# Score banks, GpSimd's share and the weights' sums in a feed-forward, attention, feed-forward block

## The chip, the cores and the metric

The kernel runs on one core of a Trainium2 chip. A core has TensorE (PE, matmuls into PSUM, with weight loads shown as PEld), VectorE (DVE), ScalarE (ACT), GpSimd (POOL) and SyncE (SP, which here issues DMAs). Each works through its own instructions in order and waits on semaphores for the others. The metric is the device time of one execution in microseconds, as the median of several runs.

## What is computed

```python
def block(x, wq, wk, wv, wo, W_up, W_gate, W_down):       # x: 16 x 256 x 256, float32
    def ffn(h):                                           # weights: 1024 x 256 (down: 256 x 1024)
        up, gate = h @ ternary(W_up).T, h @ ternary(W_gate).T
        return (silu(up) * gate) @ ternary(W_down).T
    def attn(h):                                          # 16 heads of 16
        q, k, v = split_heads(h @ wq), split_heads(h @ wk), split_heads(h @ wv)
        scores = rope(q) @ rope(k).T / sqrt(16) + causal
        return (softmax(scores) @ v) @ wo
    x = x + 0.5 * ffn(layernorm(x))
    x = x + attn(layernorm(x))
    return x + 0.5 * ffn(layernorm(x))
```

This is the reference in short. `ternary(W)` is clip(round(W / s), -1, 1) * s with s the mean of |W|.

## The kernel before

One program per engine is written out by hand; there is no scheduler. The 16 batches (256 tokens each, two tiles of 128 rows) have 8 pairs of heads each, so there are 128 attention pairs. Time is counted in **slots**: pair n has its scores, row maxima and exponentials in slot n, its split into a high and a low half (`prob_hi` on ScalarE, `prob_lo` on GpSimd) in slot n+1, and its product with v (`product_v`), after a DMA transpose of the probabilities, in slot n+3. `run_slots` calls each engine's `slot(g)` for all slots in turn; what stands in a slot, and in what order, is in the lists of calls in `slot`, one list for slots below 0 (the lead-in) and one for the rest.

Most products run in two float16 halves, a high and a low one, so each activation is made by ScalarE (`_hi`) and corrected by VectorE or GpSimd (`_lo`).

An FFN of one batch is four **rounds**, one per slot at most (`plan_rounds`): `up` and `gate` products on TensorE, `tanh` on ScalarE, `silu` and `hidden` on VectorE, `hidden_hi` on ScalarE, `hidden_lo` on GpSimd, and one slot later the `down` product. The first `AHEAD` batches' first FFN run from slot `FIRST_FFN` on; later ones start at slot 8(b - AHEAD) + `FFN1_AT`, the second FFN of batch b at 8b + `FFN2_AT`.

`OF_BATCH` places the rest: entries like ("qk0", -7, "b") put the q and k projection of tile 0 of batch b at slot 8b - 7, at the later of two places in the slot. They share one PSUM bank, `misc_ps`, in turn. `NORM_LEAD` says how many slots ahead of a norm's transposes each of its steps stands (`stats`, `mean`, `var` on VectorE, `power` on GpSimd, `shift` on VectorE, `apply` on ScalarE). `ROPE_ADD`, `ROPE_HI` and `ROW_LO` place the rotary add (GpSimd), the copies to the high rows (ScalarE) and the low rows (GpSimd), after which SyncE's queue transposes the rows of q and k.

PSUM has eight banks: up 2, gate, down, scores 2 (bank 0 the second row tile's, bank 1 the first's and the row maxima), pv and misc. Both score banks are written anew for each pair after its predecessor's exponentials (`exp_done`). The lead-in loads the weights, sums |W| on ScalarE (`sum_weights`), adds over partitions on GpSimd (`sum_all`, `max_all`) and makes the ternary weights and the float16 halves of wq, wk, wv, wo (w_hi, w_lo) on VectorE.

## Time and profile before

| | |
|---|---|
| time, median of 3 runs | 773.08 us (772.38 to 777.07) |
| the profiled execution | 772.13 us, its span 770.0 us |
| mean granted TensorE clock | 0.952 |
| mean duration of tanh, silu, hidden, hidden_hi | 681, 683, 687, 633 ns |
| up product: eight matmuls, their starts 0.11 us apart | 0.9 us |

The profile is of one execution. Its page gives each engine's busy time in the span; its other views give groups of instructions with their mean durations and the idle time before them, who waited for whom, single instructions in order of time, and busy times in chosen stretches. A matmul's duration overlaps its neighbours', so for TensorE the distance of starts counts. "issue" as releaser means that the engine waited for nothing that the profile shows.

### The profile page before, as it was taken

The page shows a single profiled execution, that of the slowest core. Times are in us where ns is not written, and L with a number is a line of the kernel's source. Part 1 is how long each engine was busy: PE and PEld are TensorE (multiplying, and loading weights), DVE is VectorE, ACT ScalarE, POOL GpSimd, SP SyncE. Part 2 cuts the span into 40 slices and gives each one's busy share as a digit, 9 for nine tenths or more (in the row PEclk, how much of TensorE's full clock was granted, in tenths as well). Part 3 has the DMA queues.
Part 4 walks back from the last instruction along what each step waited for, and adds up shares of the span by engine and source line. Part 5 has one row for each costly group of instructions (what it writes and reads, how often), then busy time and mean ns, then how long its engine had stood idle before and what let it go on. Part 6 is the DMA issues. An engine that isn't in the chain of part 4 may idle for free. (4 is left out here: it accounts for less than half of the span.)

```text
span 770.0 us, 16604 instructions
## 1 busy us (share of the span) xinstructions
PE 622.2 (81%) x5952; PEld 471.1 (61%) x5952; DVE 611.8 (79%) x1542; ACT 598.4 (78%) x1175; POOL 504.8 (66%) x440
## 2 busy tenths in 40 slices
PE   0548888768989898989898998989899696868756
PEld 0336666546767676767676776767676364646444
DVE  1857777878889998889898988888889686867643
ACT  4124578878988989888989888889899787879732
POOL 1112758766868787877868786868687767676522
PEclk9979999989999999999999999999999898989798
DMA  8500317674766666574839393947667777776520
GB/s 337 163 1 1 71 34 123 129 160 84 138 117 125 124 125 137 111 138 88 167 69 183 72 179 66 167 93 143 115 123 135 144 125 133 129 139 132 107 56 14
DMA packets 310994, 90.42 MB, mean 117 GB/s; under 512 B 301696, under 2 KB 310144, under 8 KB 310400
## 3 DMA queue, kind: packets, MB, share of 16 engines
q1 hardware_dynamic: 310336, 87.06, 58.4%
q10 hardware_dynamic: 576, 2.29, 0.8%
q8 instruction: 48, 0.79, 0.4%
q14 instruction: 34, 0.28, 0.1%
HBM read 9.63 MB, written 4.19 MB: 18 GB/s over the span
## 5 line engine op out<-in xcount | busy, mean ns | idle before, releaser
L1008 POOL TENSOR_TENSOR hid_l<-hid,hid_h 128x512 f16<-128x512 f32 x128 | 148.8, 1163 | 138.3 <-ACT hid_h L635 131.5
L615 ACT ACTIVATE prob<-score_ps,exp_bias,exp_scale 128x256 f32<-128x256 f32 (+1 forms) x512 | 223.9, 511 | 8.5 <-DVE exp_bias L868 8.3
L1003 POOL TENSOR_TENSOR prob_hl<-prob,prob_hl 128x768 f16<-128x768 f32 x128 | 210.7, 1646 | 26.5 <-ACT prob_hl L626 26.5
L386 PE MATMUL down_ps<-tern_down,hid_h 128*128 128x256 f16 x512 | 120.5, 275 | 22.9 <-POOL hid_l L1008 18.8
L386 PE MATMUL up_ps<-xt_hi,tern_up 128*128 128x256 f16 x512 | 128.2, 287 | 7.8 <-DVE tern_up L716 5.7
L386 PE MATMUL up_ps<-xt_lo,tern_up 128*128 128x256 f16 x512 | 127.6, 286 | 0.0
L386 PE MATMUL gate_ps<-xt_hi,tern_gate 128*128 128x256 f16 x512 | 122.7, 279 | 2.2 <-DVE tern_gate L716 1.8
L386 PE MATMUL gate_ps<-xt_lo,tern_gate 128*128 128x256 f16 x512 | 122.2, 278 | 0.0
L386 PE MATMUL down_ps<-tern_down,hid_l 128*128 128x256 f16 x512 | 120.2, 275 | 0.0
L630 ACT ACTIVATE tanh_b<-up_ps,tanh_scale 128x512 f32<-128x512 f32 x128 | 87.2, 681 | 39.7 <-PE up_ps L386 37.8
L895 DVE SCALAR_TENSOR_TENSOR silu_b<-tanh_b,up_ps 128x512 f32<-128x512 f32 x128 | 87.4, 683 | 34.4 <-ACT tanh_b L630 34.3
L635 ACT ACTIVATE hid_h<-hid 128x512 f16<-128x512 f32 x128 | 81.1, 633 | 41.1 <-DVE hid L904 40.9
L626 ACT ACTIVATE prob_hl<-prob 128x768 f16<-128x768 f32 x128 | 107.1, 837 | 2.0 <-DMA raw_w<-prob_hl 0.3
L904 DVE SCALAR_TENSOR_TENSOR hid<-silu_b,gate_ps 128x512 f32<-128x512 f32 x128 | 88.0, 687 | 14.0 <-PE gate_ps L386 2.4
L861 DVE TENSOR_REDUCE score_ps<-score_ps 128x2 f32<-128x512 f32 x128 | 88.8, 693 | 8.2 <-PE score_ps L413 4.9
L432 PE MATMUL pv_ps<-v_row,raw_w 128*128 128x33 f16 x1536 | 59.6, 179 | 23.3 <-DMA raw_w<-prob_hl 22.9
L432 PEld LDWEIGHTS pv_ps<-v_row,raw_w 128*128 128x128 f16 x1536 | 54.9, 97 | 36.1 <-DMA raw_w<-prob_hl 33.5
L386 PEld LDWEIGHTS down_ps<-tern_down,hid_h 128*128 128x128 f16 x512 | 50.4, 98 | 38.9 <-POOL hid_l L1008 28.0
L641 ACT ACTIVATE xhat<-xs,shift,rstd 128x256 f32<-128x256 f32 x96 | 51.9, 590 | 24.6 <-DVE shift L811 24.6
L977 POOL TENSOR_TENSOR rstd<-var_s,minus_half 128x2 f32<-128x2 f32 x48 | 33.9, 706 | 52.3 <-DVE var_s L805 52.2
L386 PEld LDWEIGHTS up_ps<-xt_hi,tern_up 128*128 128x128 f16 x512 | 52.9, 103 | 18.0 <-DVE tern_up L716 6.1
L478 PE MATMUL misc_ps<-ident_f,xhat 128*128 128x128 f32 x192 | 34.1, 307 | 34.4 <-ACT xhat L641 30.4
(95 smaller groups left out, 1335.9 us busy)
## 6 DMA issues: line engine op xcount, KB each, us to landing
xs<-x SPq DMA_DIRECT2D x16, 256.0 KB, 2.9
out<-xs SPq DMA_DIRECT2D x16, 256.0 KB, 3.0
raw_w<-prob_hl SPq DMA_TRANSPOSE x128, 3.8
raw_gate<-w_gate_t ACTq DMA_DIRECT2D x1, 1024.0 KB, 7.9
raw_up<-w_up_t SPq DMA_DIRECT2D x1, 1024.0 KB, 8.0
raw_down<-w_down_t SPq DMA_DIRECT2D x1, 1024.0 KB, 10.6
raw_w<-wqkvo ACTq DMA_DIRECT2D x1, 1024.0 KB, 13.2
cos<-rope_cos SPq DMA_DIRECT2D x1, 512.0 KB, 14.3
```

What stands on the lines that cost most here:

```text
L386: mm = pe.matmul(dst, lhs, rhs, start=flags and n == 0, stop=n == len(pairs) - 1, skip_group_check=True)
L432: mm = pe.matmul(dst, prob_t[:, n % PT_BUFS, part, block, :], v[:, keys, 2 * s + j, :], start=first, stop=True, skip_group_check=True)
L615: e = act.activation(prob[:, n % 2, at + j * width:at + (j + 1) * width], score_ps[:, 1 - tile, j * width:(j + 1) * width], ACT.Exp, bias= ...
L626: act.activation(prob_hl[:, n % 2, 0, :], prob[:, n % 2, :], ACT.Copy).then_inc(prob_h_done, 1)
L630: act.activation(tanh_b[:, n % 2, :], up_ps[:, n % 2, :], ACT.Tanh, scale=tanh_scale[:, :]).then_inc(tanh_done, 1)
L635: act.activation(hid_h[:, n % 2, :, :].rearrange("p m n -> p (m n)"), hid[:, n % 2, :], ACT.Copy).then_inc(hid_h_done, 1)
L641: a = act.activation(xhat[k][:, tile, :], x_rows(b, tile * E, E), ACT.Identity, bias=shift[k][:, tile:tile + 1], scale=rstd[k][:, tile:til ...
L861: dve.tensor_reduce(neg_max[:, 0:2], score_ps[:, 0, :].rearrange("p (j n) -> p j n", j=2), AX.X, ALU.max, negate=True)
L895: dve.scalar_tensor_tensor(out=silu_b[:, :], in0=tanh_b[:, n % 2, :], scalar=1.0, in1=up_ps[:, n % 2, :], op0=ALU.add, op1=ALU.mult).then_ ...
L904: dve.scalar_tensor_tensor(out=hid[:, n % 2, :], in0=silu_b[:, :], scalar=0.25 / X_SCALE ** 2, in1=gate_ps[:, :], op0=ALU.mult, op1=ALU.mu ...
L1003: pool.tensor_tensor(prob_hl[:, n % 2, 1, :], prob[:, n % 2, :], prob_hl[:, n % 2, 0, :], ALU.subtract).then_inc(prob_l_done, 1)
L1008: pool.tensor_tensor(hid_l[:, n % 2, :, :].rearrange("p m n -> p (m n)"), hid[:, n % 2, :], hid_h[:, n % 2, :, :].rearrange("p m n -> p (m ...
```

## The change

- **Slots.** The lead-in begins one slot earlier with one batch fewer ahead (5 for 6, so 20 rounds stand in slots -16 to 3 in place of 24 in -15 to 8, and rounds go on at slot 10, not 14). qk0, v, the rotary steps and the norms' steps move as in the tables, and every engine's calls within a slot are in a new order.
- **PSUM.** up has one bank, the scores three: the second tile alternates between banks 0 and 1, the first has bank 2. exp_bias is double. The first tile's maxima and exponentials now come first, and each tile has its own `scores_done`.
- **GpSimd** takes `norm_shift` (a product of two columns for each tile, VectorE had one instruction for both) and `pv_add`, the sum of the high and low halves of the weighted values, from two pv_norm buffers in turn.
- **Sums of the weights.** The loads are split in halves over SP's and ACT's queues. TensorE multiplies by a matrix of ones for the sums and, after a transpose, for the maxima; ScalarE sums up before the first norm, gate and down after it, and makes w_hi.
- The third norm's transposed activations lie in raw_up's memory.

```diff
--- before.py
+++ after.py
-FIRST_FFN = -15
-AHEAD = 6
+FIRST_FFN = -16
+AHEAD = 5
 FFN2_AT = 14
-FFN1_AT = 18
+FFN1_AT = 10
 PT_BUFS = 2
-MAXIMA_AT = FIRST_FFN + 3
-ALL_MAXIMA_AT = FIRST_FFN + 3
-POWERS_AT = FIRST_FFN + 4
+SUM_UP_AT = FIRST_FFN - 5
+SUM_GATE_AT = FIRST_FFN + 0
+SUM_DOWN_AT = FIRST_FFN + 0
+SPLIT_HI_AT = FIRST_FFN + 5
+TERN_DOWN_AT = FIRST_FFN + 1
+MAXIMA_AT = FIRST_FFN + 0
+TOPS_AT = FIRST_FFN + 1
+POWERS_AT = FIRST_FFN + 2
+SPLIT_LO_AT = FIRST_FFN + 7
+CASTS_AT = FIRST_FFN + 13
+PE_DOWN_AT = FIRST_FFN + 1
+PE_TURN_AT = FIRST_FFN + 1
+PE_SPREAD_AT = FIRST_FFN + 2
...
-OF_BATCH = [("norm2", -8, "a"), ("qk0", -7, "b"), ("qk1", -6, "a"), ("v", -5, "b"),
+OF_BATCH = [("norm2", -8, "a"), ("qk0", -8, "b"), ("qk1", -6, "a"), ("v", -4, "b"),
             ("attn_t", 10, "b"), ("out_proj", 11, "a"), ("norm3", 13, "b")]
...
-    1: {"stats": 4, "mean": 4, "var": 2, "power": 2, "shift": 1, "apply": 1},
-    2: {"stats": 2, "mean": 2, "var": 2, "power": 2, "shift": 1, "apply": 1},
-    3: {"stats": 2, "mean": 2, "var": 2, "power": 1, "shift": 0, "apply": 0},
+    1: {"stats": 4, "mean": 3, "var": 3, "power": 2, "shift": 2, "apply": 1},
+    2: {"stats": 3, "mean": 2, "var": 2, "power": 2, "shift": 2, "apply": 1},
+    3: {"stats": 2, "mean": 2, "var": 2, "power": 2, "shift": 2, "apply": 0},
 }
 XT_BUFS = {1: 2, 2: 1, 3: 1}
-ROPE_ADD = {-7: 0, -6: 1}
-ROPE_HI = {-6: 0, -5: 1}
-ROW_LO = {-5: 0, -3: 1}
+ROPE_ADD = {-7: 0, -5: 1}
+ROPE_HI = {-6: 0, -4: 1}
+ROW_LO = {-6: 0, -4: 1}
...
-        pv_norm = sb("pv_norm", [P, NT * 2, 2, HD])
+        pv_norm = sb("pv_norm", [P, 2, NT * 2, 2, HD])
...
-        up_ps = ps("up_ps", [P, 2, 512])
+        up_ps = ps("up_ps", [P, 512])
         gate_ps = ps("gate_ps", [P, 512])
         down_ps = ps("down_ps", [P, 512])
-        score_ps = ps("score_ps", [P, 2, 512])
+        score_ps = ps("score_ps", [P, 3, 512])
         pv_ps = ps("pv_ps", [P, 512])
         misc_ps = ps("misc_ps", [P, 512])
-        neg_max = score_ps[:, 1, 2 * P:2 * P + 4]
+        neg_max = score_ps[:, 2, 2 * P:2 * P + 4]
+        ones = pv_norm[:, 0, :, :, :].rearrange("p m a d -> p (m a d)")
+        weight_sums = [pv_ps[:, 0:1], score_ps[:, 0, 0:1], score_ps[:, 1, 0:1]]
+        w_max_row, w_max_all = pv_ps[0:4, 0:P], score_ps[:, 0, 0:4]
...
-            sp.dma_start(raw_up[:, :], w_up_t).then_inc(up_loaded, 16)
-            sp.dma_start(raw_down[:, :], w_down_t).then_inc(down_loaded, 16)
+            sp.dma_start(raw_up[:, 0:HID], w_up_t[:, 0:HID]).then_inc(up_loaded, 16)
+            sp.dma_start(raw_gate[:, 0:HID], w_gate_t[:, 0:HID]).then_inc(gate_loaded, 16)
             sp.dma_start(rows(1), x_dram[1]).then_inc(x_loaded[1], 16)
+            sp.dma_start(raw_down[:, 0:HID], w_down_t[:, 0:HID]).then_inc(down_loaded, 16)
+            sp.dma_start(raw_w[:, 0, :, :], wqkvo[:, 0, :, :]).then_inc(w_loaded, 16)
...
+            def masked_scores(dst, q, k):
+                pe.matmul(dst[:, :, -P:], ident_b[:, :], mask_b[:, :].rearrange("p (j n) -> p j n", j=2),
+                          start=True, stop=False, skip_group_check=True)
+                return pe.matmul(dst, q, k, start=False, stop=True, skip_group_check=True)
+            def scores_1(n):
                 b, s = divmod(n, SLOTS)
                 if s == 0:
                     for tile in range(NT):
                         pe.wait_ge(stk_loaded[tile], 32 * (b + 1))
-                q = q_stk[:, b % 2, s, :]
-                k = k_pad[:, b % 2, 2 * s:2 * s + 2, :]
-                pe.wait_ge(exp_done[0], n)
-                second = score_ps[:, 0, :].rearrange("p (j n) -> p j n", j=2)
-                pe.matmul(second[:, :, P:2 * P], ident_b[:, :], mask_b[:, :].rearrange("p (j n) -> p j n", j=2),
-                          start=True, stop=False, skip_group_check=True)
-                pe.matmul(second, q[:, P:2 * P], k, start=False, stop=True, skip_group_check=True)
+                if n >= 2:
+                    pe.wait_ge(exp_done[0], n - 1)
+                masked_scores(score_ps[:, n % 2, :].rearrange("p (j n) -> p j n", j=2), q_stk[:, b % 2, s, P:2 * P],
+                              k_pad[:, b % 2, 2 * s:2 * s + 2, :]).then_inc(scores_done[0], 1)
+            def scores_0(n):
+                b, s = divmod(n, SLOTS)
+                if s == 0:
+                    pe.wait_ge(stk_loaded[0], 32 * (b + 1))
                 pe.wait_ge(exp_done[1], n)
-                first = score_ps[:, 1, 0:2 * P].rearrange("p (j n) -> p j n", j=2)
-                pe.matmul(first, ident_b[:, :], mask_b[:, :].rearrange("p (j n) -> p j n", j=2),
-                          start=True, stop=False, skip_group_check=True)
-                pe.matmul(first, q[:, 0:P], k[:, :, 0:P], start=False, stop=True, skip_group_check=True
-                          ).then_inc(scores_done, 1)
+                masked_scores(score_ps[:, 2, 0:2 * P].rearrange("p (j n) -> p j n", j=2), q_stk[:, b % 2, s, 0:P],
+                              k_pad[:, b % 2, 2 * s:2 * s + 2, 0:P]).then_inc(scores_done[1], 1)
...
-                if n >= 2:
-                    pe.wait_ge(silu_done, n - 1)
-                hidden_units(up_ps[:, n % 2, :], tern_up, f, b, r).then_inc(up_done, 1)
+                pe.wait_ge(silu_done, n)
+                hidden_units(up_ps[:, :], tern_up, f, b, r).then_inc(up_done, 1)
...
+            def sum_weight(n):
+                pe.wait_ge(abs_done, n + 1)
+                pe.matmul(weight_sums[n], ones, abs_sum[:, n:n + 1], start=True, stop=True).then_inc(sums_done, 1)
...
+            def turn_maxima():
+                pe.wait_ge(wmax_done, 1)
+                pe.transpose(w_max_row, w_max[:, :], ident_f[:, :]).then_inc(wmax_turned, 1)
+            def spread_maxima():
+                pe.wait_ge(wdiag_done, 2)
+                pe.matmul(w_max_all, ones[0:4, :], w_diag[:, :], start=True, stop=True).then_inc(wmax_all, 1)
...
-                act.dma_start(raw_gate[:, :], w_gate_t).then_inc(gate_loaded, 16)
+                act.dma_start(raw_up[:, HID:2 * HID], w_up_t[:, HID:2 * HID]).then_inc(up_loaded, 16)
+                act.dma_start(raw_gate[:, HID:2 * HID], w_gate_t[:, HID:2 * HID]).then_inc(gate_loaded, 16)
+                act.dma_start(raw_down[:, HID:2 * HID], w_down_t[:, HID:2 * HID]).then_inc(down_loaded, 16)
+                act.dma_start(raw_w[:, 1, :, :], wqkvo[:, 1, :, :]).then_inc(w_loaded, 16)
                 act.dma_start(mask_f[:, :], mask).then_inc(mask_loaded, 16)
-                act.dma_start(raw_w[:, :, :, :], wqkvo).then_inc(w_loaded, 16)
...
+            def sum_weights(n, raw, junk, loaded):
+                act.wait_ge(loaded, 32)
+                act.activation(junk[:, :, :].rearrange("p a b -> p (a b)"), raw[:, :], ACT.Abs,
+                               accum_out=abs_sum[:, n:n + 1]).then_inc(abs_done, 1)
...
+            def split_weights_hi():
+                act.wait_ge(w_scales_done, 10)
+                for m in range(4):
+                    act.activation(w_hi[:, :, m, :], raw_w[:, :, m, :], ACT.Copy, scale=w_mul[:, m:m + 1]
+                                   ).then_inc(split_done, 1)
...
-            def norm_shift(k, b):
-                dve.wait_ge(rstd_done[k], b + 1)
-                dve.scalar_tensor_tensor(out=shift[k][:, :, None], in0=mv[k][:, :, 0:1], scalar=-1.0,
-                                         in1=rstd[k][:, :, None], op0=ALU.mult, op1=ALU.mult).then_inc(shift_done[k], 1)
...
-                dve.wait_ge(attn_done, n)
-                dve.tensor_tensor(pv_norm[:, :, :, :].rearrange("p m a d -> p m (a d)"), pv[:, :, 0:2 * HD],
+                if n >= 2:
+                    dve.wait_ge(attn_done, n - 1)
+                dve.tensor_tensor(pv_norm[:, n % 2, :, :, :].rearrange("p m a d -> p m (a d)"), pv[:, :, 0:2 * HD],
...
+            def norm_shift(k, b):
+                pool.wait_ge(rstd_done[k], b + 1)
+                for tile in range(NT):
+                    s = pool.tensor_scalar(shift[k][:, tile:tile + 1], mv[k][:, tile, 0:1], rstd[k][:, tile:tile + 1], -1.0,
+                                           ALU.mult, ALU.mult)
+                s.then_inc(shift_done[k], 1)
...
+            def pv_add(n):
+                b, s = divmod(n, SLOTS)
+                if s == 0:
+                    pool.wait_ge(attn_h_done, b)
+                pool.wait_ge(pv_norm_done, n + 1)
+                parts = pv_norm[:, n % 2, :, :, :].rearrange("p (n j) a d -> p n j a d", n=NT)
+                pool.tensor_tensor(attn[:, :, 2 * s * HD:2 * (s + 1) * HD].rearrange("p n (j d) -> p n j d", j=2),
+                                   parts[:, :, :, 0, :], parts[:, :, :, 1, :], ALU.add).then_inc(attn_done, 1)
...
-            def sum_all():
-                pool.wait_ge(abs_done, 2)
-                pool.partition_all_reduce(abs_sum_all[:, 0:2], abs_sum[:, 0:2], P, RADD).then_inc(abs_all, 1)
-                pool.wait_ge(abs_done, 3)
-                pool.partition_all_reduce(abs_sum_all[:, 2:3], abs_sum[:, 2:3], P, RADD).then_inc(abs_all, 1)
-            def max_all():
-                pool.wait_ge(wmax_done, 1)
-                pool.partition_all_reduce(w_max_all[:, :], w_max[:, :], P, RMAX).then_inc(wmax_all, 1)
```

GpSimd in the lead-in, from the first norm's power on, before (ISA rows without a name have no operands, those with one are the partition sums):

```order
L977 TENSOR_TENSOR rstd<-var_s,minus_half 128x2
L1039 ISA
L1039 ISA abs_sum_all<-abs_sum 128x2
L1041 ISA abs_sum_all<-abs_sum 128x1
L1008 ISA
L1008 TENSOR_TENSOR hid_l<-hid,hid_h 128x512
L977 TENSOR_TENSOR rstd<-var_s,minus_half 128x2
L1008 TENSOR_TENSOR hid_l<-hid,hid_h 128x512 x2
L1045 ISA
L1045 ISA w_max_all<-w_max 128x4
L1008 ISA
L1008 TENSOR_TENSOR hid_l<-hid,hid_h 128x512 x2
```

and in the changed kernel:

```order
L1038 TENSOR_TENSOR rstd<-var_s,minus_half 128x2
L1044 TENSOR_SCALAR shift<-mv,rstd 128x1 x2
L1087 TENSOR_TENSOR hid_l<-hid,hid_h 128x512
L1038 TENSOR_TENSOR rstd<-var_s,minus_half 128x2
L1087 TENSOR_TENSOR hid_l<-hid,hid_h 128x512
L1044 TENSOR_SCALAR shift<-mv,rstd 128x1 x2
L1087 TENSOR_TENSOR hid_l<-hid,hid_h 128x512 x3
L1038 TENSOR_TENSOR rstd<-var_s,minus_half 128x2
L1087 TENSOR_TENSOR hid_l<-hid,hid_h 128x512
L1044 TENSOR_SCALAR shift<-mv,rstd 128x1 x2
```

The four bare ISA rows and the three sums are gone, and shift stands among the norm's steps.

VectorE from the third norm's statistics to the exp_bias of the next slot (slot 8b+3), before:

```order
L795 BN_STATS stats<-xs 128x6 x2
L895 SCALAR_TENSOR_TENSOR silu_b<-tanh_b,up_ps 128x512
L800 BN_AGGR mv<-stats 128x2 x2
L904 SCALAR_TENSOR_TENSOR hid<-silu_b,gate_ps 128x512
L805 TENSOR_SCALAR var_s<-mv 128x2
L850 SCALAR_TENSOR_TENSOR v_row<-misc_ps,v_row 128x32x16
L874 RECIPROCAL inv_sum<-pv_ps 128x4
L879 TENSOR_TENSOR pv_norm<-pv_ps,inv_sum 128x128
L861 TENSOR_REDUCE score_ps<-score_ps 128x2
L863 TENSOR_REDUCE score_ps<-score_ps 128x2
L889 TENSOR_REDUCE attn<-pv_norm 128x2x32
L868 TENSOR_SCALAR exp_bias<-score_ps,exp_scale 128x4
```

and in the changed kernel:

```order
L871 BN_STATS stats<-xs 128x6 x2
L948 RECIPROCAL inv_sum<-pv_ps 128x4
L876 BN_AGGR mv<-stats 128x2 x2
L954 TENSOR_TENSOR pv_norm<-pv_ps,inv_sum 128x128
L960 SCALAR_TENSOR_TENSOR silu_b<-tanh_b,up_ps 128x512
L969 SCALAR_TENSOR_TENSOR hid<-silu_b,gate_ps 128x512
L881 TENSOR_SCALAR var_s<-mv 128x2
L937 TENSOR_REDUCE score_ps<-score_ps 128x2
L932 TENSOR_REDUCE score_ps<-score_ps 128x2
L942 TENSOR_SCALAR exp_bias<-score_ps,exp_scale 128x4
```

The v rows and the halves' sum (attn) are gone from this stretch, the inverse and the scaling of the weighted values stand ahead of silu, and the first tile's maximum ahead of the second's.

GpSimd at the same place (slots 8b+2 and 8b+3), before:

```order
L1003 TENSOR_TENSOR prob_hl<-prob,prob_hl 128x768
L985 TENSOR_TENSOR rope_r<-rope_c,rope_s 128x512
L1008 TENSOR_TENSOR hid_l<-hid,hid_h 128x512
L1003 TENSOR_TENSOR prob_hl<-prob,prob_hl 128x768
L997 TENSOR_TENSOR q_row<-rope_r,q_row 128x16x32
L997 TENSOR_TENSOR k_row<-rope_r,k_row 128x8x2x16 x2
L1008 TENSOR_TENSOR hid_l<-hid,hid_h 128x512
```

and in the changed kernel:

```order
L1082 TENSOR_TENSOR prob_hl<-prob,prob_hl 128x768
L1077 TENSOR_TENSOR attn<-pv_norm 128x2x32
L1066 TENSOR_TENSOR q_row<-rope_r,q_row 128x16x32
L1066 TENSOR_TENSOR k_row<-rope_r,k_row 128x8x2x16 x2
L1087 TENSOR_TENSOR hid_l<-hid,hid_h 128x512
L1054 TENSOR_TENSOR rope_r<-rope_c,rope_s 128x512
L1082 TENSOR_TENSOR prob_hl<-prob,prob_hl 128x768
L1077 TENSOR_TENSOR attn<-pv_norm 128x2x32
L1038 TENSOR_TENSOR rstd<-var_s,minus_half 128x2
L1044 TENSOR_SCALAR shift<-mv,rstd 128x1 x2
L1087 TENSOR_TENSOR hid_l<-hid,hid_h 128x512
```

The low rows of tile 0 have moved from slot 8b+3 to 8b+2 and rope_r of tile 1 the other way, and the halves' sum (attn), rstd and shift have come in.

## Rows read from the trace of the kernel before

**Rows 1.** The page, part 1: busy us, share of the span, instructions.

```profile
PE 622.2 (81%) x5952; PEld 471.1 (61%) x5952; DVE 611.8 (79%) x1542; ACT 598.4 (78%) x1175; POOL 504.8 (66%) x440
```

**Rows 2.** VectorE by time: start us, us, exp_bias of slots 0, 14, 94, 127.

```profile
101.31 0.22 DVE L868 TENSOR_SCALAR exp_bias<-score_ps,exp_scale 128x4 f32<-128x4 f32 x1
...
170.64 0.21 DVE L868 TENSOR_SCALAR exp_bias<-score_ps,exp_scale 128x4 f32<-128x4 f32 x1
...
579.26 0.21 DVE L868 TENSOR_SCALAR exp_bias<-score_ps,exp_scale 128x4 f32<-128x4 f32 x1
...
729.30 0.21 DVE L868 TENSOR_SCALAR exp_bias<-score_ps,exp_scale 128x4 f32<-128x4 f32 x1
```

**Rows 3.** Busy us of the engines in a steady and in a late batch.

```profile
303.70:344.20 40.50, 36.20 (x357) 27.92 (x355) 36.62 (x95) 36.39 (x74) 31.17 (x28) 0.96 0.65 125
588.50:626.30 37.80, 28.44 (x274) 20.06 (x273) 28.98 (x80) 31.17 (x63) 26.07 (x23) 0.91 0.73 133
```

**Rows 4.** Waits from 222 to 344 us: us in total, times, longest.

```profile
PE score_ps L405 <- ACT prob L615: 5.4, 5, 1.3
PEld pv_ps L432 <- DMA raw_w<-prob_hl: 5.2, 6, 2.4
ACT q_row L602 <- POOL rope_r L985: 4.3, 3, 1.4
...
ACT xhat L641 <- DVE shift L811: 3.7, 6, 0.6
```

**Rows 5.** Waits of ScalarE from 588.5 to 626.3 us, columns as above.

```profile
ACT q_row L602 <- POOL rope_r L985: 1.3, 1, 1.3
ACT v_row L585 <- PE misc_ps L386: 1.2, 1, 1.2
ACT prob L615 <- DVE exp_bias L868: 1.1, 2, 0.9
```

**Rows 6.** VectorE in the lead-in, in order of time.

```profile
20.60 2.35 DVE L716 SCALAR_TENSOR_TENSOR tern_up<-raw_up,thr_hi,below 128x2048 f16<-128x2048 f32 x1
...
28.64 0.69 DVE L904 SCALAR_TENSOR_TENSOR hid<-silu_b,gate_ps 128x512 f32<-128x512 f32 x1 [1.39 <-PE gate_ps L386]
...
36.51 1.11 DVE L811 SCALAR_TENSOR_TENSOR shift<-mv,rstd 128x2 f32<-128x2 f32 x1 [0.85 <-POOL rstd L977]
...
39.23 0.69 DVE L904 SCALAR_TENSOR_TENSOR hid<-silu_b,gate_ps 128x512 f32<-128x512 f32 x1
39.84 2.28 DVE L748 TENSOR_REDUCE w_absmax<-raw_w 128x8 f32<-128x2048 f32 x1
...
61.50 0.69 DVE L904 SCALAR_TENSOR_TENSOR hid<-silu_b,gate_ps 128x512 f32<-128x512 f32 x1 [0.15 <-PE gate_ps L386]
...
62.24 3.68 DVE L782 SCALAR_TENSOR_TENSOR w_lo<-raw_w,w_mul,w_hi 128x512 f16<-128x512 f32 x4
```

**Rows 7.** GpSimd in the lead-in; in brackets the idle time before.

```profile
47.74 0.39 POOL L1045 PARTITION_ALL_REDUCE w_max_all<-w_max  x1 [5.92 <-issue]
54.95 1.14 POOL L1008 TENSOR_TENSOR hid_l<-hid,hid_h 128x512 f16<-128x512 f32 x1 [6.82 <-issue]
```

**Rows 8.** ScalarE in the lead-in, in order of time.

```profile
9.29 1.91 ACT L568 ACTIVATE tern_up<-raw_up 128x2048 f16<-128x2048 f32 x1 [5.38 <-DMA raw_up<-w_up_t]
...
14.98 1.08 ACT L641 ACTIVATE xhat<-xs,shift,rstd 128x256 f32<-128x256 f32 x2
```

**Rows 9.** Groups by line: operands, shapes, count; busy us, mean ns; idle before.

```profile
L1003 POOL TENSOR_TENSOR prob_hl<-prob,prob_hl 128x768 f16<-128x768 f32 x128 | 210.7, 1646 | 26.5 <-ACT prob_hl L626 26.5
...
L997 POOL TENSOR_TENSOR k_row<-rope_r,k_row 128x256 f16<-128x256 f32 x64 | 41.5, 671 | 0.0
...
L889 DVE TENSOR_REDUCE attn<-pv_norm 128x64 f32<-128x128 f32 x128 | 35.5, 277 | 0.1
L811 DVE SCALAR_TENSOR_TENSOR shift<-mv,rstd 128x2 f32<-128x2 f32 x48 | 34.1, 711 | 24.6 <-POOL rstd L977 23.5
...
L977 POOL TENSOR_TENSOR rstd<-var_s,minus_half 128x2 f32<-128x2 f32 x48 | 33.9, 706 | 52.3 <-DVE var_s L805 52.2
```

331 lines of the change are left out of this document (177 added, 154 removed).

## The prediction

> **What bounds the kernel now.** I read the page's busy times first [rows 1]: TensorE, VectorE and ScalarE are each busy about 80% of the span and GpSimd 66%, so the average names no limit. So I cut the span by stage, with the 128 exp_bias instructions of VectorE, one for each attention slot, as clock [rows 2]. Slot 0 comes at 101.3 us. Slots 0 to 14 take 69.3 us. Slots 14 to 94, each with an FFN round, take 408.6 us, 40.9 for a batch of eight slots. The 33 steps from slot 94 to 127, half of them with an FFN round, take 150.0 us; a full batch there takes 37.8 [rows 3]. The tail after slot 127 takes 40.7 us.
>
> In an undisturbed batch of 40.5 us [rows 3] ScalarE is busy 36.4 us, VectorE 36.6, TensorE 36.2 and GpSimd 31.2. None is full; each waits in its own places. So the thing to read is what ends ScalarE's waits over three such batches [rows 4]: 4.3 us for rope_r from GpSimd and 3.7 for the norm's shift from VectorE, 8.0 of the 12.3 that it idles in three batches. In a late batch it is busy 31.2 of 37.8 us and waits for rope_r, for v's projection and for exp_bias [rows 5]. TensorE waits for ScalarE's exponentials before it may overwrite the only pair of score banks (5.4 us in three batches) [rows 4].
>
> The lead-in is another matter. The hidden values of FFN round 0 come at 28.64, of round 2 at 39.23, of round 5 only at 61.50 [rows 6]. Around the partition maximum at 47.74 GpSimd stands 5.92 us before it and 6.82 us after it, with "issue" as releaser [rows 7], and TensorE's down product waits for the hid_l that comes behind.
>
> **The change, part by part.**
> *Lead-in.* Weights now come in halves over two queues, up first; the partition sums and the maximum are tiny TensorE products; ScalarE sums only the up weights before the first norm, and makes w_hi. In the profile three sums run from 9.29 on and the first xhat stands behind them at 14.98 [rows 8]. The up load landed at 9.29 with x, ident, up and gate (2.3 MB) on the way since about 2.2 us; with 1.3 MB ahead it should land near 6.2. Then: sum to 8.2, xhat 1.1, transposes 1.1, xt_hi .6, xt_lo .7 to 11.9; stats and scales to 13.2; the compare and the 2.35 of ternary up [rows 6] to 16.9; ternary gate to 21.1. The maxima (2.3 us, now here) to 23.9, so hid of round 0 at 24.6 instead of 28.64. Ternary down 5 us and round 1 at 30.7; the power steps, some 1.3 us, and round 2 at about 34.5, against 39.23. From round 5 to slot 0 the kernel before took 39.8 us for ten slots, w_lo's 3.7 included [rows 2, 6], so 3.61 per slot without it. The changed kernel has 16 slots ahead of slot 0, 14 of them from round 2 on: 34.5 + 14 x 3.61 + 3.7 = 88.7, **12.6 us** earlier than 101.3. The stall around the maximum is inside this, and so is the extra slot. Bounds: 7 us if each of those slots takes 3.98, the average with w_lo in it; 17 as far on the other side.
>
> A sentence of the Trainium skill speaks against this part: GPSIMD Engine Reference, section 4.1, names GpSimd for a reduction along partitions. Its section 2.1 speaks for it: the first call to freshly loaded code pays about 6 us (5.95) with no visible instruction. By that figure two loads around the maximum are 12 us; the trace has 12.7, so it agrees.
>
> *Score banks.* The second tile's scores alternate between two banks, so they can be written while the previous exponentials run; the first tile's bank is free earlier, its exponentials now going first. The up product pays: it has one bank, and up of round n+1 waits for silu of round n. From up's end, tanh, silu and the next up make a loop of 2.3 us by the durations in the table above, shorter than the average slot of 5.1, so I cost it at nothing; the cover is the slot's other work, and it is gone only where silu itself is late.
>
> *Shift on GpSimd.* On VectorE the 48 shifts cost 34.1 us, 711 ns each [rows 9], and 1.11 us where hid_l runs beside them [rows 6]. That goes. GpSimd gets two single-column instructions for each, between the .18 that the sizes below leave for no element and the .71 of rstd [rows 9]; I take .2, as rstd's is a power. Three norms a batch: 1.2 us (1.1 to 4.2).
> The Trainium skill's SBUF — State Buffer, section Who interferes with whom, says that a VectorE instruction with two SBUF inputs and a GpSimd instruction that reads SBUF block each other; the 1.11 agrees. By it the new add on GpSimd blocks none of VectorE's frequent instructions, which have a PSUM input, and the sum would not change.
>
> *Halves added on GpSimd.* VectorE loses 128 x 277 ns [rows 9]. GpSimd's cost by size: .67 at 256 elements, 1.65 at 768 [rows 9], so .18 and 1.9 ns an element, which gives the 1.15 of hid_l at 512 [rows 7]: .30 for 64. Eight a batch: 2.4 us. Bound above: .67 each, 5.4 us. The skill's GPSIMD Engine Reference, section 4.1, has two-input work at twice VectorE's time; by that it would be .55 each, and 2 us a batch more. The second pv_norm buffer takes the add off VectorE's path: the scaling of slot n waits for the add of n-2 only.
>
> *Order.* rope_r is made one slot before its reader, v has left the slot behind out_proj, qk0 shares norm2's slot, and shift stands a slot or two ahead of its apply. So in the steady batches ScalarE's waits for rope_r (4.3 / 3 = 1.43) and shift (1.23) go [rows 4]. Against that, GpSimd, with its 3.6 us more, comes to 34.8 us, 90% of the shorter batch, as full as VectorE is now, and it stands between ScalarE and the transposes. I give back 30% of those 3.6, 1.06; that share is a choice, no row has it. Per batch 1.43 + 1.23 - 1.06 = **1.6 us**, in ten batches **16 us**. Ends: nothing, and 4.1 (ScalarE's idle time).
> Slots 0 to 13: 14/8 of 1.6, and one FFN round fewer. A round's presence costs (40.5 - 37.8) / 4 = .7 us. Together **3.5 us**.
> Late batches: of the waits in [rows 5] rope_r's 1.3 and v_row's 1.2 are what the order attacks and exp_bias's 1.1 what the third bank does, 3.6 us. GpSimd goes from 26.1 [rows 3] to 29.7, and the chains through the norms stay, so I take half, 1.8, in 4.2 batches: **7.6 us**.
> *Tail.* Its chain is one norm, transposes and four FFN rounds, in which the order changes little: 0, plus or minus 1.5.
>
> **Sum.** 12.6 + 3.5 + 16 + 7.6 = 39.7 us off the profiled span of 770.0: 730.3. That execution took 772.13, 2.1 us outside its span, and lies 0.95 under the median of 773.08. 730.3 + 2.1 + 1.0 = 733.4, say **733**. Own range 718 to 747.
>
> **Rivals.**
> *Only the lead-in pays* (15%). Three engines are at 36 of 40.5; when ScalarE's waits go, the same microseconds may reappear as waits for TensorE or GpSimd one step on. For it: every engine is near 90%. Against: the waits for rope_r and shift come of placement, not of throughput. Then 12.6 + .7 and some 4 late, 17.3: 756.
> *ScalarE runs full* (12%). With the banks decoupled each steady batch nears its 36.4 busy: 37, ten times 3.9, with 5, 12.6 and 12 elsewhere, 68.6: 705.
> *The single up bank chains the engines* (10%). silu now stands behind the scaling of the weighted values, which waits for their product, and so for the transposed probabilities (5.2 us in three batches, 1.7 in one [rows 4]); with one up bank such a wait holds the next up product, and ScalarE behind it. The shorter waits of the order (2.7) would be used up by 1.7 that now reach ScalarE and as much again where that product, now behind up, comes late. With a microsecond a batch lost, the steady part adds 10 and the lead-in's 12.6 is nearly gone: 770, no difference.
> *GpSimd becomes the bound* (7%), the slower side. If the add costs .67 and a shift instruction .7, a batch gets 5.4 + 4.2 = 9.6 us more: 31.2 + 9.6 = 40.8, and with 4 us of its waits for ScalarE left 44.8, 4.3 over now. Ten batches lose 43 us, the lead-in and the late part give 17 back: 799. It decides from some 5.3 us a batch more (36.5 + 4 = 40.5), so an add of .45 with shifts of .3. The line through the sizes speaks against it, the nested access pattern of the add for it.
>
> **How the numbers follow.** The forecast has 56%. The range 708 to 757 takes in it and the first rival and reaches most of the way to the second; it leaves out the last two. A difference within 1% (7.7 us) is about what this kernel's measurement can't tell from none. Faster by more: 56 + 15 + 12 = 83%; within: 10%; slower: 7%.
>
> **What would show it.** Slot 0's exp_bias at 85 to 94 us, and no idle of 6 us with "issue" on GpSimd in the rounds of the lead-in; steady batches of 38.5 to 39.5 us, late ones near 36; ScalarE's waits for rope_r and shift near zero, GpSimd busy 34 to 36 a batch; the add near 300 ns and shift near 200. The forecast is wrong if steady batches stay at 40.5, if up waits for silu on TensorE, or if GpSimd's new instructions cost twice what I took.

## The result: 5.3% faster, and where it came from

The changed kernel takes 732.9 us (median of 4 runs, 729.7 to 737.9), the kernel before, on the same chip, 774.5 us (4 runs, 772.4 to 777.1). The ratio is 0.9467, with a 95% interval of 0.9404 to 0.9531. The prediction was 733 us. The profiled execution took 732.3 us, 730.5 of it in the span.

The page, part 1, of the changed kernel: busy us, share of the span and instructions of each engine.

```profile
PE 607.2 (83%) x5961; PEld 477.7 (65%) x5961; DVE 569.8 (78%) x1368; ACT 590.8 (81%) x1179; POOL 565.4 (77%) x661
```

Against [rows 1], VectorE lost 42 us of work and GpSimd gained 61, and the span fell by 39.5. No engine is nearer to full than 83%, so again the average says nothing of the limit, and the stages have to be read.

VectorE by time, changed kernel: exp_bias of slots 0, 14, 94 and 127, to be laid beside [rows 2].

```profile
91.27 0.22 DVE L942 TENSOR_SCALAR exp_bias<-score_ps,exp_scale 128x4 f32<-128x4 f32 x1
...
155.90 0.22 DVE L942 TENSOR_SCALAR exp_bias<-score_ps,exp_scale 128x4 f32<-128x4 f32 x1
...
542.12 0.22 DVE L942 TENSOR_SCALAR exp_bias<-score_ps,exp_scale 128x4 f32<-128x4 f32 x1
...
686.98 0.22 DVE L942 TENSOR_SCALAR exp_bias<-score_ps,exp_scale 128x4 f32<-128x4 f32 x1
```

| stage | before | changed | forecast of the difference | measured |
|---|---|---|---|---|
| up to slot 0 | 101.3 | 91.3 | -12.6 | -10.0 |
| slots 0 to 14 | 69.3 | 64.6 | -3.5 | -4.7 |
| slots 14 to 94 | 408.6 | 386.2 | -16 | -22.4 |
| slots 94 to 127 | 150.0 | 144.9 | -7.6 | -5.1 |
| tail | 40.7 | 43.5 | 0 | +2.8 |
| sum | 770.0 | 730.5 | -39.7 | -39.5 |

The sum hit because its misses cancel, which is luck and not precision: the steady batches gave 6.4 us more than forecast, the lead-in, the late batches and the tail 7.9 less, slots 0 to 14 1.2 more.

Busy us by engine in windows of the changed kernel (columns as in [rows 3]: window, length, PE, PEld, DVE, ACT, POOL with instructions, granted TensorE clock, DMA share, GB/s): a steady batch, a late batch, the tail.

```profile
279.40:318.20 38.80, 35.87 (x375) 29.22 (x373) 33.86 (x84) 35.88 (x74) 34.96 (x42) 1.00 0.72 130
549.90:586.30 36.40, 28.32 (x274) 21.11 (x273) 26.43 (x69) 30.70 (x63) 29.24 (x35) 0.91 0.78 142
687.00:730.50 43.50, 28.80 (x224) 20.74 (x221) 16.33 (x33) 13.87 (x24) 14.54 (x17) 0.79 0.15 31
```

A steady batch is 1.9 us shorter than in the kernel before (38.6 us against 40.55 in most batches; the batch shown above happens to take 38.8), though ScalarE still works 35.9 us in it; what left is waiting. GpSimd is at 35.0, VectorE at 33.9. Waits of the changed kernel over three steady batches, 202.3 to 318.2 us (total, times, longest), to be laid beside [rows 4]:

```profile
POOL hid_l L1087 <- ACT hid_h L702: 9.4, 12, 1.3
...
DVE silu_b L960 <- ACT tanh_b L697: 5.6, 9, 1.5
PE misc_ps L504 <- ACT xhat L708: 4.6, 3, 1.6
ACT tanh_b L697 <- PE up_ps L409: 3.0, 3, 1.0
ACT attn_h L641 <- PE misc_ps L504: 2.4, 3, 0.8
```

ScalarE's waits for rope_r and for the shift are gone from these batches, and TensorE no longer waits for score banks in them. Most of what ScalarE still waits for (the last two rows, 5.4 of its 8.1 us) has one place in every batch, the slot in which attn is transposed (timeline of the changed kernel, the third slot of the batch from 279.4; idle time before in brackets):

```profile
291.30 0.32 POOL L1077 TENSOR_TENSOR attn<-pv_norm 128x64 f32<-128x64 f32 x1
...
291.77 0.63 PE L504 MATMUL misc_ps<-ident_f,attn 128*128 128x128 f32 x4 [0.60 <-POOL attn L1077]
...
292.43 0.60 ACT L641 ACTIVATE attn_h<-misc_ps 128x512 f16<-128x512 f32 x1 [0.79 <-PE misc_ps L504]
...
296.20 0.69 ACT L697 ACTIVATE tanh_b<-up_ps,tanh_scale 128x512 f32<-128x512 f32 x1 [1.01 <-PE up_ps L409]
```

The last add of the batch, now on GpSimd behind the low half of the probabilities, ends at 291.62; TensorE had waited 0.60 us for it, ScalarE waits for the transposes, then for the next up product. That slot takes 6.46 us, the average is 4.83. The wait for the add came with the change, and it is the first thing to try below.

The groups of the two operations that moved (columns as in [rows 9]):

```profile
L1077 POOL TENSOR_TENSOR attn<-pv_norm 128x64 f32<-128x64 f32 x128 | 41.2, 322 | 6.8 <-DVE pv_norm L954 6.3
...
L1044 POOL TENSOR_SCALAR shift<-mv,rstd 128x1 f32<-128x1 f32 x96 | 24.8, 274 | 4.1
```

Lead-in of the changed kernel, VectorE by time, beside [rows 6]:

```profile
14.72 0.75 DVE L871 BATCH_NORM_STATS2 stats<-xs 128x6 f32<-128x256 f32 x2 [1.63 <-DMA xs<-x]
...
17.14 2.35 DVE L788 SCALAR_TENSOR_TENSOR tern_up<-raw_up,thr_hi,below 128x2048 f16<-128x2048 f32 x1
...
26.96 0.69 DVE L969 SCALAR_TENSOR_TENSOR hid<-silu_b,gate_ps 128x512 f32<-128x512 f32 x1
...
37.89 0.69 DVE L969 SCALAR_TENSOR_TENSOR hid<-silu_b,gate_ps 128x512 f32<-128x512 f32 x1
```

Ternary up comes 3.5 us earlier, at 17.14, and would have come at 15.5 but for the statistics of batch 1, which stand ahead of it and wait 1.63 us for their rows. Round 0 is at 26.96 (forecast 24.6), round 2 at 37.89 (34.5); the fourteen slots from there to 91.27, with w_lo, take 53.4 us (forecast 54.2).

### The profile page after: what moved, and what is told of

Read it like the earlier page. It is cut to its first block, busy times and chain, and to the rows that moved or that the text cites. A ratio compares the mean times of both kernels' runs of the same rounds, so it can differ in the third digit from the quotient of the medians.

```text
span 730.5 us, 16813 instructions
## 1 busy us (share of the span) xinstructions
PE 607.2 (83%) x5961; PEld 477.7 (65%) x5961; DVE 569.8 (78%) x1368; ACT 590.8 (81%) x1179; POOL 565.4 (77%) x661
## 4 chain that ended last, share of the span: by engine, by line
ACT 32%; DVE 14%; issue 11%; POOL 11%; PE 8%; DMA 4%; SPq 1%; DVEq 0%; POOLq 0%; ACTq 0%
ACT prob L682 12%; POOL prob_hl L1082 5%; ACT tanh_b L697 5%; ACT prob_hl L693 4%; DMA raw_w<-prob_hl 4%; PE misc_ps L504 4%; POOL hid_l L1087 3%; ACT xhat L708 3%; ACT hid_h L702 3%; DVE silu_b L960 2%; DVE hid L969 2%; DVE xs L886 2%; DVE stats L871 1%; DVE attn_l L897 1%; PE up_ps L409 1%
## 5 line engine op out<-in xcount | busy, mean ns | idle before, releaser
L682 ACT ACTIVATE prob<-score_ps,exp_bias,exp_scale 128x128 f32<-128x128 f32 (+1 forms) x512 | 224.0, 515 | 5.9 <-DVE exp_bias L942 5.9
L419 PE MATMUL score_ps<-k_pad,q_stk 128*128 128x512 f16 (+1 forms) x256 | 80.3, 337 | 0.0
L417 PE MATMUL score_ps<-mask_b,ident_b 128*128 128x256 bf16 x256 | 71.8, 280 | 7.9 <-ACT prob L682 7.9
L409 PE MATMUL up_ps<-raw_up,tern_up 128*128 128x256 f16 x512 | 71.4, 286 | 4.5 <-DVE raw_up L897 4.1
L459 PEld LDWEIGHTS pv_ps<-v_row,raw_w 128*128 128x128 f16 x1536 | 57.3, 97 | 20.4 <-DMA raw_w<-prob_hl 11.5
L409 PE MATMUL gate_ps<-raw_up,tern_gate 128*128 128x256 f16 x512 | 69.7, 281 | 0.0
L409 PE MATMUL up_ps<-xt_hi,tern_up 128*128 128x256 f16 x256 | 61.5, 279 | 9.0 <-DVE tern_up L788 4.7
L504 PE MATMUL misc_ps<-ident_f,xhat 128*128 128x128 f32 x192 | 32.2, 294 | 43.5 <-ACT xhat L708 41.1
L937 DVE TENSOR_REDUCE score_ps<-score_ps 128x2 f32<-128x256 f32 x128 | 54.5, 426 | 12.8 <-PE score_ps L419 11.7
```

The costliest lines, as they stand in the source:

```text
L409: mm = pe.matmul(dst, lhs, rhs, start=flags and n == 0, stop=n == len(pairs) - 1, skip_group_check=True)
L419: return pe.matmul(dst, q, k, start=False, stop=True, skip_group_check=True)
L459: mm = pe.matmul(dst, prob_t[:, n % PT_BUFS, part, block, :], v[:, keys, 2 * s + j, :], start=first, stop=True, skip_group_check=True)
L682: e = act.activation(prob[:, n % 2, at + j * width:at + (j + 1) * width], score_ps[:, n % 2 if tile else 2, j * width:(j + 1) * width], AC ...
```

## Experiments: one part undone at a time

All times are medians, and the ratios are taken to runs of the kernel before on the same chip (its medians there were 772.8 to 775.7 us; 774.5 is the one beside the changed kernel). A difference of two or three us between rows of the table can therefore come of the chip and the runs. The stages are read from each run's exp_bias rows as above. "Steady" is a batch between slots 24 and 48, the mean of three.

| kernel | us | ratio to before, 95% | up to slot 0 | slots 14 to 94 | steady |
|---|---|---|---|---|---|
| before | 774.5 | 1 | 101.3 | 408.6 | 40.55 |
| changed | 732.9 | 0.9467 (0.9404 to 0.9531) | 91.3 | 386.2 | 38.6 |
| shift on VectorE, head of slot | 754.3 | 0.9728 (0.9693 to 0.9763) | 92.3 | 396.6 | 39.7 |
| shift on VectorE, later | 752.7 | 0.9706 (0.9662 to 0.9750) | 91.0 | 408.2 | 40.8 |
| add on VectorE | 732.8 | 0.9453 (0.9419 to 0.9488) | 90.7 | 388.2 | 38.8 |
| old banks | 797.6 | 1.0293 (1.0251 to 1.0334) | 90.3 | 428.3 | 42.8 |
| all-reduce on GpSimd | 750.1 | 0.9679 (0.9642 to 0.9716) | 105.1 | 386.6 | 38.7 |
| parts in the old order | 787.8 | 1.0167 (1.0124 to 1.0209) | 104.6 | 413.5 | 40.9 |
| add made twice | 742.1 | 0.9568 (0.9527 to 0.9610) | 89.6 | 390.4 | 39.1 |
| attn_t a slot later | 720.4 | 0.9288 (0.9247 to 0.9329) | 91.1 | 379.3 | 37.8 |
| + statistics later | 723.0 | 0.9345 (0.9299 to 0.9390) | 90.7 | 381.2 | 38.1 |
| + add on VectorE | 713.2 | 0.9214 (0.9180 to 0.9249) | 90.6 | 376.8 | 37.6 |
| add on VectorE, statistics back | 713.5 | 0.9218 (0.9187 to 0.9249) | 91.5 | 373.7 | 37.3 |
| add first in GpSimd's slot | 760.8 | 0.9829 (0.9795 to 0.9862) | 92.0 | 409.9 | 41.0 |

### The shift back on VectorE, at the head of the slot

```diff
-                for tile in range(NT):
-                    s = pool.tensor_scalar(shift[k][:, tile:tile + 1], mv[k][:, tile, 0:1], rstd[k][:, tile:tile + 1], -1.0,
-                                           ALU.mult, ALU.mult)
+                dve.scalar_tensor_tensor(out=shift[k][:, :, None], in0=mv[k][:, :, 0:1], scalar=-1.0,
+                                         in1=rstd[k][:, :, None], op0=ALU.mult, op1=ALU.mult).then_inc(shift_done[k], 1)
```
In VectorE's slot it stands behind the FFN's residual add and ahead of the row maxima, one slot after the power; in `NORM_LEAD` the shift's entries go from 2 to 1. So the shift also comes a slot later than in the changed kernel, here and in the next experiment.

> The changed kernel with one part undone: the shift of every norm is again one instruction of VectorE, one slot after the power, and leaves GpSimd. Theory (the part of the gain between slots 14 and 94 comes from ScalarE no longer finding the shift and the rotated rows late): ScalarE's wait for the shift comes back, 1.2 us a batch in the kernel before, and the stretch from slot 14 to slot 94 (386.2 us) grows by 4 to 12 us, the whole by 5 to 20. Rival (the order of the slots alone took the wait away, whoever computes the shift): within 3 us of the changed kernel, and no wait for the shift above 0.3 us a batch.

Measured: 754.3 us, 21 more than the changed kernel, 10.4 of it between slots 14 and 94 and 10.1 in slots 94 to 127. Timeline of this kernel, where the slot that took 4.59 us now takes 6.5:

```profile
225.81 0.70 POOL L1048 TENSOR_TENSOR rstd<-var_s,minus_half 128x2 f32<-128x2 f32 x1 [0.29 <-DVE var_s L881]
226.48 1.15 POOL L1089 TENSOR_TENSOR hid_l<-hid,hid_h 128x512 f16<-128x512 f32 x1
226.54 1.11 DVE L887 SCALAR_TENSOR_TENSOR shift<-mv,rstd 128x2 f32<-128x2 f32 x1 [0.81 <-POOL rstd L1048]
227.57 0.42 DVE L943 TENSOR_REDUCE score_ps<-score_ps 128x2 f32<-128x256 f32 x1
```

The shift waits 0.81 us for rstd and then takes 1.11 us for two elements a partition, ending with the hid_l that GpSimd started a moment before; 148 ns is its shortest in this kernel. The row maxima stand behind both: 1.9 us late, and the exponentials with them. Later slots give back some of it, and a steady batch is 1.0 us longer. What I had expected, a wait of ScalarE for the shift, is a small part of it: 0.5 us in three steady batches. In slots 94 to 127 there is none, while ScalarE's wait for exp_bias is 14.2 us there against 5.6 in the changed kernel. The size was nearly right (21 us for the 5 to 20 expected), the victim was another.

### The shift on VectorE, behind the row maxima

The same kernel with the instruction moved in VectorE's slot from ahead of the row maxima to behind exp_bias.

> The changed kernel with the shift on VectorE as in the run with the shift at the head of the slot (21 us slower than the changed kernel), but placed behind the row maxima and exp_bias of the same slot. Theory of place (what cost the 21 us was that the row maxima stood behind a VectorE instruction that waited 0.81 us for GpSimd's rstd and then took 1.11 us): nearly all of it comes back, within 5 us of the changed kernel. Rival (the engine itself costs: an instruction of VectorE that takes 1.1 us beside GpSimd, and one more hop between engines): 10 to 20 us slower than the changed kernel.

Measured: 752.7 us. The theory of place fell: the row maxima no longer stand behind it, and still 20 us are lost, now almost all between slots 14 and 94 (408.2 us against 386.2). Timeline of this kernel:

```profile
323.07 1.63 POOL L1084 TENSOR_TENSOR prob_hl<-prob,prob_hl 128x768 f16<-128x768 f32 x1
323.12 1.61 DVE L887 SCALAR_TENSOR_TENSOR shift<-mv,rstd 128x2 f32<-128x2 f32 x1
...
324.76 1.09 ACT L708 ACTIVATE xhat<-xs,shift,rstd 128x256 f32<-128x256 f32 x2 [1.72 <-DVE shift L887]
```

Here rstd was long done, VectorE waited for nothing, and the instruction ran 1.61 us, exactly as long as the prob_hl beside it on GpSimd; ScalarE waited 1.72 us for it. With the 0.15 us that it takes alone it would have ended 1.46 us sooner, so most of that wait is of the engine. The place has a share too: the shift now stands in the slot of its reader, and a shift of GpSimd at this later place was not tried. In both experiments the instruction, which has both inputs in SBUF, ended with the GpSimd instruction beside it. The Trainium skill's SBUF — State Buffer, section Who interferes with whom, says that a VectorE instruction with two SBUF inputs contends with a GpSimd instruction that reads SBUF; the 1.61 beside 1.63 agrees. On GpSimd the shift stands in line behind rstd and costs 0.27 us a piece.

### The add back on VectorE

```diff
-                pool.tensor_tensor(attn[...], parts[:, :, :, 0, :], parts[:, :, :, 1, :], ALU.add).then_inc(attn_done, 1)
+                dve.tensor_reduce(attn[...], pv_norm[:, n % 2, :, :, :].rearrange("p (n j) a d -> p n j d a", n=NT), AX.X, ALU.add
+                                  ).then_inc(attn_done, 1)
```
It stands behind silu, and the two buffers stay.

> The changed kernel with one part undone: the halves of the weighted values are added on VectorE again (behind silu, still from two buffers), not on GpSimd. Theory (VectorE's relief is worth time): 8 adds of 0.28 us a batch come back to VectorE, which is busy 33.9 of 38.8 us a batch; 0.3 to 1 us a batch, so 5 to 16 us slower. Rival (GpSimd, busy 35.0 of 38.8 us, is what bounds the changed kernel): it loses 8 adds of 0.32 us a batch, and the kernel is 3 to 15 us faster.

Measured: 732.8 us, no difference; both sides of my expectation fell. GpSimd is busy 2.3 us a batch less (35.0 to 32.7), VectorE only 0.8 more (33.9 to 34.7), and the batch takes 38.8 us against 38.6. In this order neither engine's sum decides. It does once the order changes, below.

### The old banks in the new order

```diff
-                if n >= 2:
-                    pe.wait_ge(exp_done[0], n - 1)
-                masked_scores(score_ps[:, n % 2, :]...
+                pe.wait_ge(exp_done[0], n)
+                masked_scores(score_ps[:, 0, :]...
```
with up in two banks again.

> The changed kernel with one part undone: two score banks and two banks for the up product, as before, in the changed order. The scores of a pair's second tile then wait for the exponentials of the pair ahead. Theory (the third bank is what lets the scores stand first in TensorE's slot): TensorE waits for ScalarE's exponentials in every slot, 0.2 to 0.5 us a slot over 128 slots, 25 to 65 us slower. Rival (the banks are worth nothing by themselves): within 4 us.

Measured: 797.6 us, 65 more than the changed kernel and 23 more than before. Waits from 217 to 346 us, three batches:

```profile
PEld score_ps L417 <- ACT prob L681: 17.8, 21, 1.1
DVE score_ps L936 <- PE score_ps L419: 17.3, 21, 1.9
PE score_ps L417 <- ACT prob L681: 16.1, 24, 1.4
```

TensorE waits in every slot, 24 times 0.67 us, for the exponentials of the pair ahead, and VectorE's row maxima wait behind it. I had expected 0.2 to 0.5 us a slot and 25 to 65 us in all, so it came out at the upper end. So this order can't be had without the third bank. The bank that up gave for it costs nothing that shows in the steady batches: in three of them the changed kernel has no wait of up for silu. In the lead-in it has two:

```profile
27.00 0.37 PE L409 MATMUL up_ps<-xt_hi,tern_up 128*128 128x256 f16 x1 [0.67 <-DVE silu_b L960]
...
49.63 0.27 PE L409 MATMUL up_ps<-xt_hi,tern_up 128*128 128x256 f16 x1 [1.55 <-DVE silu_b L960]
```

What these 2.2 us of waiting cost at slot 0 was not tried.

### The partition sums and maxima back on GpSimd

```diff
-                pe.matmul(weight_sums[n], ones, abs_sum[:, n:n + 1], start=True, stop=True).then_inc(sums_done, 1)
+                    pool.partition_all_reduce(abs_sum_all[:, n:n + 1], abs_sum[:, n:n + 1], P, RADD).then_inc(sums_done, 1)
```
and the same for the maxima, with which VectorE's reduction of four rows and its diagonal go too; nothing else moves.

> The changed kernel with one part undone: the sums and the maxima over the partitions are taken by GpSimd's all-reduce again, at the same places of the order, TensorE's five instructions for them are gone. Theory: GpSimd's idle issue time of 6 us ahead of the first all-reduce of maxima, and of the next instruction after it, comes back; the first exp_bias (91.3 us) comes 8 to 13 us later and the whole is 8 to 13 us slower, nothing else changes. Rival (the lead-in is set by the loads and by VectorE's ternary work, GpSimd is beside it): within 3 us.

Measured: 750.1 us, 17 more. The first exp_bias comes at 105.1 us, 13.8 later. GpSimd of this kernel in the lead-in:

```profile
40.13 0.39 POOL L1131 PARTITION_ALL_REDUCE w_max_all<-w_max  x1 [6.41 <-issue]
47.23 0.73 POOL L1039 TENSOR_TENSOR rstd<-var_s,minus_half 128x2 f32<-128x2 f32 x1 [6.71 <-issue]
```

The two idle stretches of 6 us with "issue" as releaser, of [rows 7], are back around the maximum, 13.1 us in all. They are not the whole of the 13.8, though the numbers are close. Following the hidden values, round 0 is 3.4 us late already (30.32 us against 26.96), round 2 4.6 (42.49 against 37.89) and round 3 13.8 (54.87 against 41.06), and it stays at that. The first 3.4 us belong to the sums. ScalarE has the up weights' sum ready at 8.96 us, but the first all-reduce runs at 18.25, and VectorE waits for it:

```profile
18.25 1.14 POOL L1127 PARTITION_ALL_REDUCE abs_sum_all<-abs_sum  x3 [11.68 <-ACT tern_down L621]
```
```profile
18.69 0.15 DVE L776 TENSOR_SCALAR tern_scale<-abs_sum_all 128x1 f32<-128x1 f32 x1 [3.69 <-POOL abs_sum_all L1127]
```

The profile puts GpSimd's wait down to the third sum; the kernel asks only for the first before the first all-reduce, so it doesn't say what held that one. Of the stall around the maximum about 10 us reach the rounds; the rest falls in time in which GpSimd would have waited anyway. My theory (8 to 13 us at slot 0 and in all, nothing else) was somewhat low on the first and wrong on "nothing else". The remaining 3.6 us of this profile lie in slots 94 to 127 (148.5 us against 144.9), which this edit doesn't touch; over the other kernels that stage moves by some us for small shifts in time, so I don't explain them. At slot 0 the all-reduces cost more than the stage's entire gain of 10.0, which also pays for one more slot ahead of slot 0.

### The parts in the old order

The kernel before, with three score banks and one for up, the shift on GpSimd behind the power, and the add on GpSimd behind the low half of the probabilities, from two buffers.

> The kernel before with the parts but neither the new order nor the new lead-in: three score banks and one bank for up, the shift on GpSimd right behind the power, and the halves added on GpSimd (behind the low half of the probabilities) from two buffers; tables, slot lists, loads and partition sums stay as they were. Theory (the slots' order is what turns the parts into time): 0 to 10 us faster than before; the wait for rope_r of 1.4 us a batch stays, that for the shift goes. Rival (the parts make the gain by themselves, the order is nothing): the batch of 40.6 us falls to 38.6 us as in the changed kernel, 25 to 30 us faster.

Measured: 787.8 us, 12 slower than the kernel before beside it (775.7). Both expectations fell. The wait for rope_r of 1.4 us a batch stays as expected, that for the shift falls from 3.7 to 1.4 us in three batches, and a new one comes. Timeline of this kernel where attn is transposed:

```profile
318.45 0.31 POOL L993 TENSOR_TENSOR attn<-pv_norm 128x64 f32<-128x64 f32 x1
...
318.90 0.63 PE L478 MATMUL misc_ps<-ident_f,attn 128*128 128x128 f32 x4 [1.12 <-POOL attn L993]
319.57 0.60 ACT L574 ACTIVATE attn_h<-misc_ps 128x512 f16<-128x512 f32 x1 [1.01 <-PE misc_ps L478]
```

It is the stall of the changed kernel, larger: 1.12 us of TensorE, 1.01 of ScalarE, and the slot grows from 5.83 to 6.94 us. Slots 14 to 94 take 4.9 us more than before, so the stall may eat what the shift gives, which is argued and not shown; 3.3 us more go up to slot 0, 6.7 in slots 94 to 127 and 2.3 in the tail, which I didn't follow. Which of the parts (banks, shift, add) loses in the old order was not taken apart. So these parts by themselves lose, and the order without its bank loses more: bank and order pay only together.

### The add made twice

```diff
+                pool.tensor_tensor(dup[:, n % 2, :, :]..., parts[:, :, :, 0, :], parts[:, :, :, 1, :], ALU.add)
                 pool.tensor_tensor(attn[...], parts[:, :, :, 0, :], parts[:, :, :, 1, :], ALU.add).then_inc(attn_done, 1)
```

> The changed kernel with GpSimd's add of the halves made twice for every pair (the first goes to a buffer that nobody reads): 0.32 us more a pair, 2.6 us a batch on an engine that is busy 35.0 of 38.8 us. Theory (GpSimd is fully in the loop only at a few slots; taking the add away changed nothing): 0 to 8 us slower. Rival (GpSimd is the bound now, at every slot): 2.6 us a batch, 30 to 40 us slower.

Measured: 742.1 us, 9 more, between my two sides (0 to 8 and 30 to 40). The intervals of the two ratios just touch; the steady batches, all within 0.2 us of each other, tell more. One of them:

```profile
240.80:279.80 39.00, 35.78 (x374) 29.15 (x373) 33.92 (x83) 35.94 (x74) 37.07 (x50) 1.00 0.71 129
```

GpSimd is now busy 37.1 of 39.0 us, and the batch grew by 0.43 us for 2.1 us more of work. So GpSimd is not the bound at 95%: about a fifth of this added work shows in the batch. I had taken 30% in the prediction.

### attn_t a slot later

```diff
-            ("attn_t", 10, "b"), ("out_proj", 11, "a"), ("norm3", 13, "b")]
+            ("attn_t", 11, "a"), ("out_proj", 11, "b"), ("norm3", 13, "b")]
-    3: {"stats": 2, "mean": 2, "var": 2, "power": 2, "shift": 2, "apply": 0},
+    3: {"stats": 1, "mean": 1, "var": 1, "power": 1, "shift": 1, "apply": 0},
```

> A candidate: the transposes of attn from place b of slot 10 to place a of slot 11, the output projection to place b of slot 11, and the statistics, mean, variance, power and shift of norm 3 one slot later (12). In the changed kernel TensorE waits 0.60 us in every batch for GpSimd's last add, ScalarE 0.79 us for attn_t and 1.01 us for the next up. Theory: the slot of 6.46 us falls to about 5.5, 1 us a batch, 10 to 16 us faster than the changed kernel. Rival (the residual add and norm 3 come too late for the FFN behind them): its apply waits for the shift, and it is 5 to 20 us slower than the changed kernel.

Measured: 720.4 us, 12.5 less than the changed kernel (8.7 between the two profiled executions). The same place in its timeline:

```profile
251.94 0.32 POOL L1077 TENSOR_TENSOR attn<-pv_norm 128x64 f32<-128x64 f32 x1
...
253.05 0.60 PE L504 MATMUL misc_ps<-ident_f,attn 128*128 128x128 f32 x4
253.70 0.59 ACT L641 ACTIVATE attn_h<-misc_ps 128x512 f16<-128x512 f32 x1
```

The add ends at 252.26, 0.8 us before TensorE comes to it, and no row has a wait. The slot takes 5.21 us instead of 6.46; some 0.4 us of that come back in the next slots, and a steady batch falls from 38.6 to 37.8. In slots 94 to 127 TensorE's wait for the add falls from 9.9 us to 1.2, and they take 141.4 us instead of 144.9.

### Four variants of it

With the statistics, mean and variance of norm 1 one slot later (`{"stats": 3, "mean": 2, "var": 2, ...}` for norm 1):

> The candidate with attn_t and the output projection later (12.5 us faster than the changed kernel), and beside it the statistics, mean and variance of norm 1 one slot later, so that at the start VectorE turns the up weights to ternary ahead of the statistics of batch 1, for whose rows it waited 1.6 us. Theory: the first exp_bias 1.5 us earlier, the rest unchanged: 0 to 3 us faster than that candidate, not to be told from noise in the whole time. Rival (the later statistics make norm 1's apply late in the loop): 2 to 10 us slower.

Measured: 723.0 us. Round 0's hid comes at 23.9 us instead of 26.8, 2.9 earlier, and round 2's still 1.6 earlier (36.1 against 37.7), yet slot 0's exp_bias at 90.7 instead of 91.1. What takes up the rest was not followed. The intervals of the two overlap; no gain shows.

The same with the add on VectorE:

> The same candidate with both moves, and the add of the halves back on VectorE behind silu. In the changed kernel the side of the add made no difference; TensorE's wait for GpSimd's add ahead of attn_t is gone in this candidate. Theory (neither engine bounds by its sum): within 4 us of the candidate with the add on GpSimd. Rival (with the stall gone, the busier of the two decides; GpSimd at 35 of 38 us): 4 to 12 us faster with the add on VectorE.

Measured: 713.2 us, 10 less, so the theory fell and the rival holds in this order. Its batches take 37.64 us against 38.12. The slot ahead of norm 3's transposes, first with the add on GpSimd, then with it on VectorE:

```profile
223.59 1.33 POOL L1066 TENSOR_TENSOR k_row<-rope_r,k_row 128x256 f16<-128x256 f32 x2
223.91 1.03 DVE L881 TENSOR_SCALAR var_s<-mv 128x2 f32<-128x2 f32 x1
225.03 0.70 POOL L1038 TENSOR_TENSOR rstd<-var_s,minus_half 128x2 f32<-128x2 f32 x1
...
227.60 0.63 PE L504 MATMUL misc_ps<-ident_f,xhat 128*128 128x128 f32 x4 [1.58 <-ACT xhat L708]
```

```profile
220.94 1.30 POOL L1080 TENSOR_TENSOR k_row<-rope_r,k_row 128x256 f16<-128x256 f32 x2
222.08 0.18 DVE L881 TENSOR_SCALAR var_s<-mv 128x2 f32<-128x2 f32 x1
222.34 0.70 POOL L1052 TENSOR_TENSOR rstd<-var_s,minus_half 128x2 f32<-128x2 f32 x1
...
225.28 0.63 PE L504 MATMUL misc_ps<-ident_f,xhat 128*128 128x128 f32 x4 [1.10 <-ACT xhat L708]
```

TensorE waits 1.58 us a batch for norm 3's xhat in the one and 1.10 in the other, 0.48 less, and that is the difference of the batches. The rows suggest why: measured from the batch's first exp_bias (200.64 and 198.82 us), GpSimd, with the add in its queue, comes 0.83 us later to the low halves of the keys (k_row). VectorE's var_s starts at the same point of the batch in both, and in both it ends with the second of them; it takes 1.03 us, not 0.18, and rstd, shift and xhat stand behind it. That chain is read from the rows, not tested by itself.

The same with the add first in GpSimd's slot:

> The same candidate with both moves, and GpSimd's add of the halves ahead of the low half of the probabilities (1.65 us) in its slot, not behind it. Theory: nobody waits for the add once attn_t stands a slot later, and GpSimd would now stand idle for VectorE's scaling of the weighted values, which comes late in the slot, with the low half of the probabilities and the turning DMA behind it: 10 to 40 us slower than the candidate. Rival: within 3 us.

Measured: 760.8 us, 38 more, as expected. From 202 to 316 us, a little under three batches, GpSimd stands 6.9 us in five waits for VectorE's scaling, and the low halves of the probabilities and of hid come behind it. An instruction that must wait holds up all that is ready behind it on its engine.

The fourth leaves norm 1's statistics where the changed kernel has them:

> The changed kernel with attn_t, the output projection and norm 3's chain one slot later and the add of the halves back on VectorE; norm 1's statistics stay where the changed kernel has them. It tells whether the fastest run so far (713.2 us, with norm 1's statistics later) owes anything to those statistics: the two runs that differ by them alone stood at 0.9345 and 0.9288 of the kernel before. Theory (they are worth nothing): 710 to 716 us. Rival (they cost 2 to 4 us in the loop): 707 to 711 us.

Measured: 713.5 us (6 runs, 712.8 to 715.4), ratio 0.9218. Its batches take 37.33 us, a little less than the 37.64 with the later statistics, and the whole is the same. The theory (710 to 716 us) holds. A steady batch:

```profile
237.80:275.10 37.30, 35.51 (x375) 29.17 (x373) 34.70 (x91) 35.80 (x74) 32.65 (x34) 1.00 0.72 135
```

ScalarE is busy 35.8 of 37.3 us, 96%. With the 713.2 us above, from which it can't be told, this is the fastest version, 2.6% under the changed kernel and 7.8% under the kernel before.

## Why the prediction was right, and where its steps were off

*Lead-in, forecast -12.6, measured -10.0.* The mechanism holds: the idle around the maximum is gone, and with the all-reduces put back slot 0 comes 13.8 us later. The prediction left out one half of it: 3.4 of the 13.8 us are there before the maximum, with the sums. Mis-sized were the steps ahead of round 2 (34.5 forecast, 37.89 measured): I let the up load land at 6.2 (the sum starts at 7.52), and left out the wait of 1.63 us for batch 1's rows ahead of ternary up. The slots after it came out as worked out, 53.4 against 54.2, though up waits for silu in two of the lead-in's rounds. The variant that took the 1.63 away had 0.4 us left of it at slot 0, so an earlier start isn't enough; what else sets the end of the lead-in is open.

*Score banks, forecast nothing by themselves.* Right for up's single bank in the steady batches, which have no wait for silu. The prediction named such a wait as a sign that it is wrong, and it came twice, 2.2 us in all, in the lead-in. But I had put the order's gain in its own term without saying that it can't exist without the bank, and undoing the banks costs 65 us. The rival of the single up bank, which took a microsecond off every batch, is refuted.

*Shift, forecast a wait of ScalarE of 1.23 us a batch.* The size is near (20 us over the kernel when undone, 1.0 to 2.2 us a steady batch), but the reason is wider: VectorE's instruction ended with the GpSimd instruction beside it (1.11 us beside 1.15, 1.61 beside 1.63), and whoever is behind it waits, the row maxima or the norm. I quoted the rule for the price of one instruction, and did not cost what stands behind it. On GpSimd it costs 0.27 a piece, not 0.2.

*Add, forecast .30 us.* Measured 0.32. That relieving VectorE of it is worth nothing in this order was not foreseen; in my sum it had no gain of its own, only GpSimd's give-back.

*Order, forecast -1.6 us a batch.* Measured -2.2, and this sum does not add up. ScalarE's two waits went as said (1.43 and 1.23). The give-back of 30% was too high: the doubled add shows a fifth, 0.3 us a batch less. And I missed that the later add would hold TensorE where attn is transposed: 0.7 to 0.8 us a batch, as the kernel with that place moved shows. With both put right the forecast would be some 1.2 us, so about 1 us a batch of the gain has no term. Of this, 0.3 us is that a few batches of the kernel before are longer than 40.55 (its mean is 40.86). The rest may be the waits for score banks and for the transposed probabilities (5.4 and 5.2 us in three batches [rows 4]), which the prediction gave no gain and which the same list of the changed kernel no longer has; no run tells their share. Nor does a run undo single moves of the order, of rope_r, v or qk0: that the order counts is shown only by the parts without it.

*Late batches, forecast -7.6, measured -5.1; tail, forecast 0, measured +2.8.* In the late batches TensorE waits 9.9 us in four times, 3.3 at most, for the add ahead of attn's transposes, the wait that the prediction missed; with attn_t a slot later it is 1.2 and the stage is 3.5 us shorter, more than the 2.5 that were lacking. In the tail the granted clock was lower, 0.79 against 0.89 in the kernel before. This row is the tail of the kernel before:

```profile
729.30:770.00 40.70, 25.58 (x222) 19.27 (x219) 16.92 (x36) 13.26 (x23) 12.37 (x11) 0.89 0.15 33
```

TensorE's busy time for nearly the same instructions is 3.2 us longer in the changed kernel, but that doesn't explain the 2.8. The last kernel above, at 0.86 in its tail and with 26.96 us of TensorE, 1.4 more than before, still takes 43.2 us. Some 0.4 us is the shift's two instructions on GpSimd: from the last rstd's start to its xhat pass 1.33 us against 0.92. The rest is open, and so is why the clock is lower.

*The rivals.* That only the lead-in pays is refuted by the steady batches, 38.6 us against 40.55. That GpSimd becomes the bound is refuted by the doubled add. "ScalarE runs full" was not this kernel's case, but with two further moves it is nearly reached: 37.3 us a batch, 713 us, where I had put 37 and 705.

## What to carry to other kernels

Undoing one part at a time gives 21, 0, 65 and 17 us here, 103 in all for a gain of 42, and the parts in the old order lose 12: what a placement, a buffer or an engine's choice is worth depends on the others, so undo each from the new kernel and also put the parts alone into the old. When an operation is moved to another engine, look at once for the one reader that has no slack for it; here it was one transposition a batch, and moving that by a slot gave 12.5 us more. Where an engine takes its work in order, place first what is ready (38 us here). Try a tiny step between two SBUF tiles on the engine that makes its input; here that was worth 20 us. When a cost put back comes near the length of a stall, follow the rounds one by one before calling the stall the cause.

## What the runs showed of the hardware

A VectorE instruction of two elements a partition, 0.15 us alone, took 1.11 us beside a GpSimd instruction of 1.15 and 1.61 beside one of 1.63. Not only instructions with two tensor inputs do so: in the changed kernel w_mul, with one tensor and one scalar column, takes 1.07 us where it took 0.17 before, from 35.19 on, beside the hid_l of GpSimd that starts at 35.09, and the cast of ident_b takes 1.18 us (0.22 before), beside the next hid_l below.

```profile
35.09 1.15 POOL L1087 TENSOR_TENSOR hid_l<-hid,hid_h 128x512 f16<-128x512 f32 x1 [2.01 <-ACT hid_h L702]
35.19 1.07 DVE L846 TENSOR_SCALAR w_mul<-w_inv 128x4 f32<-128x4 f32 x1
...
79.73 1.29 POOL L1087 TENSOR_TENSOR hid_l<-hid,hid_h 128x512 f16<-128x512 f32 x1 [0.94 <-ACT hid_h L702]
79.91 1.18 DVE L771 CAST ident_b<-ident_f 128x128 bf16<-128x128 f32 x1
```

GpSimd is held as well: in the changed kernel its rstd, 0.71 us at other places, takes 2.75 from 30.33 us on, beside VectorE's 3.13 us of tern_down that end at 32.52.

A single all-reduce across the partitions on GpSimd, 0.39 us long, stood between 13.1 us of idle time (6.41 ahead and 6.71 behind), where a transposition, a reduction of four rows and two tiny instructions more did the same work with no such idle on GpSimd.
